# A transformer layer with routed experts on one core: eight expert tiles between the last attention pieces, routing batches of 4, 2 and 2

## What is computed

```python
x = x + self_attention(layernorm(x))             # 16 heads of 16, rotary embedding on 8 of each 16
x = x + cross_attention(layernorm(x), ctx, mask) # 16 heads, values and keys are ctx itself
x = x + experts(layernorm(x))
# experts: 8 of them, 256 -> 1024 -> 256, exact gelu; each token goes to its best two
router = x @ router_w.T + router_b + 0.1 * language_weights
top_p, top_i = top_k(softmax(router), 2);  top_p /= top_p.sum()
out = sum_k top_p[k] * (gelu(x @ w1[top_i[k]] + b1) @ w2[top_i[k]] + b2)
```

## Time and profile before

| | |
|---|---|
| median of 3 runs | 758.14 us (757.3 to 761.05) |
| the profiled execution | 760.69 us, span 758.7 us |
| PE busy | 644.1 us, 85% of the span |
| ACT, DVE, POOL busy | 53%, 46%, 38% |
| mean granted clock of PE | 0.928 |

### The profile page before, as it was taken

How to read it: one execution, slowest core, us unless ns; L and a number is a source line. 1 busy time by engine, 2 the same in 40 slices (tenths; PEclk the granted TensorE clock), 3 DMA queues, 4 the chain that set the end, 5 groups by cost and what they waited for, 6 DMA issues and landing times.

```text
span 758.7 us, 15126 instructions
## 1 busy us (share of the span) xinstructions
PE 644.1 (85%) x4858; PEld 515.5 (68%) x4858; DVE 348.7 (46%) x793; ACT 401.5 (53%) x870; POOL 284.9 (38%) x543
## 2 busy tenths in 40 slices
PE   4476798798998989999977413999999999999996
PEld 3354576475766666666634313999999999999995
DVE  1386777586786877777751440121211212212121
ACT  3443657467575777777654122545455454454551
POOL 3232305335144464643247352233324334243332
PEclk9697999899999999999998555999999999999998
DMA  5637466546677577776957901222222122221221
GB/s 127 132 96 153 96 136 150 138 121 148 134 175 157 141 152 163 178 186 143 308 131 141 226 29 37 23 37 44 31 41 42 29 43 36 36 43 29 43 30 21
DMA packets 57596, 78.25 MB, mean 103 GB/s; under 512 B 12877, under 2 KB 51152, under 8 KB 54448
## 3 DMA queue, kind: packets, MB, share of 16 engines
q1 hardware_dynamic: 48552, 66.61, 38.2%
q0 software_dynamic: 8512, 10.26, 8.6%
q10 hardware_dynamic: 456, 0.42, 0.2%
HBM read 54.52 MB, written 22.35 MB: 101 GB/s over the span
## 4 chain that ended last, share of the span: by engine, by line
PE 56%; DMA 11%; POOL 11%; issue 8%; SPq 7%; DVE 4%; ACT 3%; POOLq 0%; DVEq 0%; ACTq 0%
PE experts_psum L1218 19%; PE experts_psum L1232 17%; DMA xs<-in_x 5%; PE attention_psum L572 4%; POOL lists L1060 4%; PE attention_psum L532 4%; PE attention_psum L601 4%; PE attention_psum L545 3%; SPq L437 3%; DMA weights<-parts 2%; PE attention_psum L483 2%; POOL weights L1111 2%; SPq L443 1%; POOL rstd L1033 1%; PE experts_psum L1206 1%
## 5 line engine op out<-in xcount | busy, mean ns | idle before, releaser
L895 DVE TENSOR_REDUCE neg_max<-attention_psum 128x2 f32<-128x512 f32 x256 | 167.3, 684 | 57.7 <-PE attention_psum L532 57.3
L683 ACT ACTIVATE weights<-attention_psum 128x512 f32<-128x512 f32 x256 | 149.4, 596 | 68.2 <-PE attention_psum L545 67.2
L1218 PE MATMUL experts_psum<-xT,w1t 128*128 128x128 f32 x1248 | 146.9, 276 | 0.0
L1218 PEld LDWEIGHTS experts_psum<-xT,w1t 128*128 128x128 f32 x1248 | 143.8, 193 | 0.1
L1232 PE MATMUL experts_psum<-weights,hidT 128*128 x624 | 141.0, 379 | 0.0
L1270 ACT ACTIVATE hidT<-experts_psum,b_sb 128x128 f32<-128x128 f32 x312 | 89.6, 369 | 85.7 <-PE experts_psum L1218 85.6
L1361 POOL DMA_INDIRECT out<-y_gated,list x39 | 62.3, 1596 | 179.6 <-DVE y_gated L1335 176.5
L1232 PEld LDWEIGHTS experts_psum<-weights,hidT 128*128 128x128 f32 x624 | 115.7, 190 | 14.1
L532 PE MATMUL attention_psum<-weights 99*128 99x256 bf16 x512 | 101.9, 282 | 23.3 <-DMA weights<-parts 12.4
L1330 DVE TENSOR_TENSOR y<-experts_psum,b_sb 128x256 f32<-128x256 f32 x39 | 16.6, 425 | 207.6 <-PE experts_psum L1232 207.6
L545 PE MATMUL attention_psum<-weights 102*128 102x256 bf16 x512 | 101.3, 281 | 1.6 <-ACT weights L683 1.0
(11 more groups left out here) (158 smaller groups left out, 709.2 us busy)
## 6 DMA issues: line engine op xcount, KB each, us to landing
parts<-weights SPq DMA_DIRECT2D x96, 128.0 KB
weights<-parts SPq DMA_DIRECT2D x32, 384.0 KB
weights<-parts SPq DMA_DIRECT2D x32, 256.0 KB
weights<-in_L_ffn_w SPq DMA_DIRECT2D x8, 1024.0 KB, 11.9
weights<-parts SPq DMA_DIRECT2D x32, 128.0 KB
w_sb<-in_L_ffn_w SPq DMA_DIRECT2D x8, 512.0 KB, 3.7
weights<-in_L_ffn_w SPq DMA_DIRECT2D x8, 512.0 KB, 8.3
xs<-in_x SPq DMA_DIRECT2D x8, 256.0 KB, 8.1
```

The costliest lines, as they stand in the source:

```text
L683: act.activation(m.p[:, u % P_RING, :], m.b_bank[u % B_RING], ACT.Exp, scale=SCALE[ORDER[u // H][0]]).then_inc(m.b_free[u % B_RING], 1)
L895: v.tensor_reduce(m.neg_max[:, :, h:h + 1], m.a_bank[u % A_RING].rearrange("p (t k) -> p t k", t=T), AXX, ALU.max, negate=True).then_inc(m ...
L1218: last = pe.matmul(r.hT_bank[j % 2][:, c * P:(c + 1) * P], r.w1t[j % 2][:, k, c * P:(c + 1) * P], r.xT[j % 2][:, k, :], start=(k == 0), st ...
```

## The change

**Batches** end after cross units 3, 5 and 7: eight, four and four tiles. The list writes of the first stand in slots 240 to 254, two in every second slot, those of the second in 272 to 278, those of the third all in 304.

**Two tables.** After the first batch the kernel takes only full tiles of 128: at least eight exist, whatever the routing. DVE computes the table of these eight in slot 241, and that of the other 31 in slot 304, from the final counts less what the eight have taken.

**One stream.** The experts' functions are gone; their parts are pieces too (`TILES_AT`), placed by hand between slots 261 and 304, and from slot 304 on one tile per slot in the old order. `up` and `down` are cut into halves. The list writes of each batch have a semaphore of their own, the stores of the first four sequences too, so that the early tiles wait only for these.

**Memory.** The experts' buffers lie over attention's: w1's copies over the values, the hidden rows over the first four sequences' `xs`, the other rows over constants of attention; the banks of up are the four score banks, and the x transposes and down's results use the attention ring of three banks. Because down's end has to free a ring bank and to tell ACT, PE signals the second by an instruction of its own (`pe.sem_inc`).

```diff
-BATCH_ENDS = (5, 7, 8)
+BATCH_ENDS = (4, 6, 8)
+EARLY = 8
+assert BATCH_ENDS[0] * S * TOPK - E * (P - 1) > (EARLY - 1) * P
-AFTER_BATCH = ((39, "softmax"), (39, "soft_exp"), (40, "choose"), (42, "count"), (42, "gate_exp"), (43, "gates"), (43, "places"))
-LISTED_AT, LISTED_EVERY = 44, 2
+AFTER_BATCH = (((39, "softmax"), (39, "soft_exp"), (40, "choose"), (42, "count"), (42, "gate_exp"), (43, "gates"),
+                (43, "places"), (44, "counted"), (45, "table")),
+               ((39, "softmax"), (39, "soft_exp"), (40, "choose"), (42, "count"), (42, "gate_exp"), (43, "gates"),
+                (43, "places")),
+               ((39, "softmax"), (39, "soft_exp"), (40, "choose"), (40, "gate_exp"), (42, "count"), (43, "gates"),
+                (43, "places"), (44, "counted"), (44, "table")))
+LISTED_AT = ((44, 2), (44, 2), (44, 0))
+TILES_AT = ((261, "list", 0), (261, "list", 1), (261, "list", 2), (261, "list", 3), (262, "w1t", 0),
+            (264, "list", 4), (264, "list", 5), (264, "list", 6), (264, "list", 7),
+            (264, "gather", 0), (264, "gather", 1), (264, "gather", 2), (268, "xturn", 0), (270, "xturn", 1),
+            (272, "gather", 3), (274, "gather", 4), (276, "gelu_table", 0), (277, "up_a", 0), (277, "w1t", 1), (282, "up_b", 0),
+            (284, "up_a", 1), (285, "w1t", 2), (285, "xturn", 2), (287, "gather", 5), (288, "up_b", 1),
+            (288, "down_a", 0), (288, "down_b", 0), (292, "moved_y", 0), (292, "w1t", 3), (293, "xturn", 3),
+            (294, "gather", 6), (295, "add", 0), (297, "up_a", 2), (298, "up_b", 2), (299, "down_a", 1),
+            (299, "down_b", 1), (301, "up_a", 3), (301, "moved_y", 1), (301, "xturn", 4), (301, "w1t", 4),
+            (302, "up_b", 3), (302, "add", 1), (303, "gather", 7), (303, "down_a", 2), (303, "down_b", 2),
+            (304, "moved_y", 2), (304, "add", 2))
+STEADY, STEADY_AT = 3, 304
...
+    for j in range(STEADY, N_TILES):
+        for name, ahead in (("list", 4), ("gather", 4), ("w1t", 2), ("xturn", 2), ("up_a", 1), ("up_b", 1),
+                            ("down_a", 0), ("down_b", 0), ("moved_y", 0), ("add", 0)):
+            for k in range(j + ahead, j + ahead + 1):
+                if k < N_TILES and (name not in ("list", "gather") or k > EARLY + 1):
+                    slots[STEADY_AT + j - STEADY].pieces.append((name, TILE, k))
+            if name == "list" and j == EARLY - 4:
+                slots[STEADY_AT + j - STEADY].pieces += [(name, TILE, EARLY), (name, TILE, EARLY + 1)]
+            if name == "gather" and j in (EARLY - 3, EARLY - 2):
+                slots[STEADY_AT + j - STEADY].pieces.append((name, TILE, j + 3))
...
+            elif name == "list":
+                if n == 0:
+                    sp.wait_ge(m.s_listed[0], 16 * TOPK * T * BATCH_ENDS[0])
+                    sp.wait_ge(m.s_routed, 1)
+                if n == EARLY:
+                    for b in range(1, len(BATCH_ENDS)):
+                        sp.wait_ge(m.s_listed[b], 16 * TOPK * T * (BATCH_ENDS[b] - BATCH_ENDS[b - 1]))
+                    sp.wait_ge(m.s_routed, 2)
...
+            elif name == "up_a":
+                if n == 0:
+                    for w in range(A_RING):
+                        pe.wait_ge(m.a_free[w], len(ORDER) * H // A_RING)
+                if n == 1:
+                    for w in range(B_RING):
+                        pe.wait_ge(m.b_free[w], len(ORDER) * H // B_RING)
+                pe.wait_ge(*m.emptied(("xturn", TILE, n)))
...
+                up(n, 0)
+            elif name == "down_a":
+                if n == 0:
+                    pe.wait_ge(m.s_w2, 16 * E)
...
+            elif name == "down_b":
+                pe.wait_ge(m.s_gelu, 2 * n + 2)
+                down(n, 1, expert).then_inc(m.fills(("down_a", TILE, n)), 1)
+                pe.sem_inc(m.s_down, 1)
...
+            elif name == "gelu_table":
+                act.activation(m.scratch[:, :], m.half[:, 0:1], ACT.Gelu)
+            elif name == "w1t":
...
+                if n < 2:
+                    act.wait_ge(m.s_values, (len(ORDER) - V_RING // 2 * (1 - n)) * H)
+                else:
+                    act.wait_ge(m.s_up, 2 * (n - 1))
...
+            elif name == "gather":
+                pool.wait_ge(m.s_list[n % LIST_RING], 16 * (n // LIST_RING + 1))
...
+                if n >= X_RING:
+                    pool.wait_ge(*m.filled(("xturn", TILE, n - X_RING)))
+            elif name == "add":
...
+                pool.wait_ge(m.s_gated, n + 1)
+                if n > 0:
+                    pool.wait_ge(m.s_add, 16 * n)
```

More of the change, by code:

```diff
@@ L181, in schedule @@
         for table, lag in (((SELF_AT, CROSS_AT)[a], 0), (BOTH_AT, 0), ((AFTER_SELF, AFTER_CROSS)[a], LAG), (AFTER, LAG)):
-            for at, *piece in table + (AFTER_BATCH if table is AFTER_CROSS and n + 1 in BATCH_ENDS else ()):
+            if table is AFTER_CROSS and n + 1 in BATCH_ENDS:
+                table = table + AFTER_BATCH[batch_of(n)[0]]
+            for at, *piece in table:
                 if piece[0] != "x" or n > 1:
@@ L309, in for_attention, with for_experts @@
         self.o_bank = banks[:, 7, :]
+        self.hT_bank = [banks[:, b:b + 2, :].rearrange("p b n -> p (b n)")
+                        for b in (RING_BANKS, RING_BANKS + A_RING)]
+    def for_experts(self):
+        rows = Arena(self.over)
+        self.x_rows, self.xT = [rows([P, D]) for _ in range(X_RING)], [rows([P, KC, P]) for _ in range(2)]
+        self.y, self.y_gated = rows([P, D]), [rows([P, D]) for _ in range(2)]
+        self.list = rows([P, N_TILES, 2])
+        self.tile_expert, self.tile_row = rows([P, N_TILES], I32), rows([P, N_TILES], I32)
+        self.expert_f, self.skipped = rows([P, N_TILES]), rows([P, N_TILES])
+        self.past, self.skip = rows([P, N_TILES, E - 1]), rows([P, N_TILES, E - 1])
+        self.tiles_i, self.tiles_i2 = rows([P, E], I32), rows([P, E], I32)
+        self.tiles, self.ends, self.gap, self.full = (rows([P, E]) for _ in range(4))
+        self.early = rows([P, E + 1])
+        self.sums = rows([P, E, E])
+        heads = Arena(self.all_v)
+        self.w1t = [heads([P, KC, F]) for _ in range(2)]
+        stored = Arena(self.xs[:, 0:BATCH_ENDS[0] * T, :].rearrange("p n d -> p (n d)"))
+        self.hidT = [stored([P, FC, P]) for _ in range(2)]
     def signals(self):
@@ L332, in signals @@
         self.s_ctx_load = [sem(f"ctx_load{i}") for i in range(2)]
-        self.s_out, self.s_rows = sem("stored_out"), sem("stored_rows")
+        self.s_out, self.s_rows = ([sem(f"stored_{x}{i}") for i in range(2)] for x in ("out", "rows"))
         self.s_dve, self.s_pool = sem("dve_chain"), sem("pool_chain")
@@ L356, in fills, with stored @@
         return self.ring_full[self.plan.use[piece] % RING_BANKS]
+    def stored(self, sems, n):
+        first = BATCH_ENDS[0] if n >= BATCH_ENDS[0] else 0
+        return sems[n >= BATCH_ENDS[0]], 16 * (n - first + 1)
     def rows_of(self, n):
@@ L367, in sync_attention @@
 def sync_attention(m, x, ctx_in, mask, wq, bq, wk, bk, wv, bv, wo, bo, w_fc, router_w, router_b, lang_w, lang_b,
-                   w1, b1, w2, b2, rope, out, rows, parts, neg):
+                   w1, b1, w2, b2, rope, out, rows, parts, neg, table):
     sp, plan = m.nc.sync, m.plan
@@ L574, in values, with up, down @@
         last.then_inc(m.s_values, TOGETHER)
+    def up(j, half):
+        for c in range(half * FC // 2, (half + 1) * FC // 2):
+            for k in range(KC):
+                last = pe.matmul(m.hT_bank[j % 2][:, c * P:(c + 1) * P], m.w1t[j % 2][:, k, c * P:(c + 1) * P],
+                                 m.xT[j % 2][:, k, :], start=(k == 0), stop=(k == KC - 1))
+        last.then_inc(m.s_up, 1)
+    def down(j, half, expert):
+        for c in range(half * FC // 2, (half + 1) * FC // 2):
+            last = pe.matmul(m.bank_of(("down_a", TILE, j))[:, 0:D], m.hidT[j % 2][:, c, :],
+                             m.w2_sb[:, bass.ds(expert, 1), c, :].rearrange("p a n -> p (a n)"),
+                             start=(c == 0), stop=(c == FC - 1))
+        return last
     for slot in plan.slots:
@@ L867, in gates @@
         chain.done(v.tensor_scalar(m.total[:, tiles], m.ratio[:, tiles], 1.0, None, ALU.add))
-        then(v.tensor_tensor, m.before[:, b + 1, :], m.before[:, b, :], m.batch[:, :], ALU.add)
-        m.routed = chain.n
+        v.wait_ge(chain.sem, chain.n)
+        v.tensor_tensor(m.before[:, b + 1, :], m.before[:, b, :], m.batch[:, :], ALU.add).then_inc(m.s_before, 1)
         then(v.reciprocal, gate[0], m.total[:, tiles])
@@ L990, in vector_attention, with pool_attention @@
                                 ALU.add).then_inc(m.frees(piece), 1)
-def pool_attention(m, table):
+def pool_attention(m, table, rows, out):
     pool, plan = m.nc.gpsimd, m.plan
@@ L1377, in build @@
         sync_attention(m, x, ctx_in, mask, wq, bq, wk, bk, wv, bv, wo, bo, w_fc, router_w, router_b, lang_w, lang_b,
-                       w1, b1, w2, b2, rope, out, rows, parts, neg)
```

(3 more changed lines are left out.)

417 lines of the change are left out of this document (193 added, 224 removed).

## The result

The changed kernel took 747.87 us (median of 4 runs, 746.08 to 749.77), the kernel before, run beside it, 758.30 us (757.3 to 761.05): ratio 0.9857, 95% interval 0.982 to 0.9895. That is 10.4 us faster, where 26 were forecast, and outside the range at its upper end. The profiled execution took 748.79 us (2.0 us around its span of 746.8), 11.9 us less than the one of before.

What follows compares the result with a forecast made beforehand. PE was taken to bound the experts' stretch at 7.25 us a tile, so only tiles computed before 468 us gain. Steps 1 to 5 gave 495.3 − 469.4 = 25.9 us off 758.14: 732 us forecast, range 719 to 746.

Steps and rivals of the forecast that it cites:

- Step 1: First batch's choice and early table among the scores: PE comes 4.8 us late to slot 250, at 382.5 us.
- Step 2: List writes delay POOL in slot 250: PE waits 8.9 us, plus 2.3 at lower clock; slot 258 at 403.1.
- Step 3: Slots 258 to 276: 20.4 us (17 to 23), ending at 423.5 us.
- Step 4: Tail up to the first down: down 0 waits for w2, starts at 446.9 us and ends at 450.4.
- Step 5: From down 0's end to the transpose of tile 5: 19.0 us, reaching it at 469.4 us.
- S: Time of the transpose of tile 5, first instruction of the steady order: forecast 469.4 us, 495.3 in the old kernel.
- Covered, with 1 us to spare: Last batch's lists: gather 8 can be back at about 490 us, PE wants it at 491.2.
- An up would wait about 1 us once: Experts' buffers over attention's: without cover an up waits for a copy, about 1 us once; costed at nothing.
- POOL does not hold up the scores: List writes keep ahead and the wait in slot 250 is 0: 721 us; chance 0.20.
- the rival of chance 0.25: The clock stays low as far as the transpose of tile 5: 744 us; chance 0.25.
- A price on every tile: The extra signal at each down's end costs up to 0.87 us on each of 39 tiles: 766 us; chance 0.05.
- It does not do what it says: PE waits for late data ahead of tile 0, w2 or lists; early tiles run after the hole: 758 us; chance 0.03.

Runs made afterwards that it cites:

- e1: Changed kernel with the first batch's list writes spread around POOL's parts of the maxima; ratio to before 0.9804.
- e12: Kernel of e7 with six of the last batch's eight list writes left out; 740.55 us, ratio to before 0.969.
- e5: Changed kernel with every early-tile piece from slot 272 on put 29 slots later, behind the last unit; 753.72 us, ratio to before 0.9854.
- e9: Kernel before with only its batch ends changed, to 4, 6, 8; 770.65 us against 764.4, ratio 1.0074.
- e11: Changed kernel with the last four w2 blocks ahead of the stores and gathers 8 and 9 one step earlier; 745.54 us, ratio to before 0.974.
- e7: Changed kernel with last four w2 blocks and gathers 8 and 9 earlier, and down 2's result copied ahead of the late table; 745.33 us, ratio 0.9735.
- e14: Kernel of e7 run again as control on chip E; 745.35 us, ratio to before 0.9734.
- e13: Kernel of e7 with the last batch's list writes split, four in slot 304 and four in 305, behind add 3; ratio to before 0.9748.
- c2: The changed kernel unaltered, run on chip D; 753.12 us, ratio to before 0.9828.
- e2: Changed kernel with the last four blocks of w2 issued ahead of the stores of cross unit 6; ratio to before 0.9756.
- e8: Kernel of e7 with two more blocks of w2 earlier, in slot 260; 748.34 us, ratio to before 0.9758.

## Why the prediction was wrong, point by point

**Step 1** had the choice right (a wait of 2.82 us at 365.05, moved and not added). Its price for the early table was too low: the table cost a wait of 3.36 us and not 1.7, and the clock was at 0.67 between 366 and 374 us, behind the wait of 2.82 us; PE arrived at slot 250 at 386.8 us (392.73 − 5.90) and not at 382.5. **Step 2** was right in its mechanism and its place (slot 250 at 391.4 forecast, 392.73 measured), and its wait was 5.9 us and not 8.9, since PE came later. That slot 258 met the forecast so well (403.1 and 402.85) is in part luck: it came 10.1 us behind slot 250 where 9.4 + 2.3 were charged, which made up for the 1.3 us that slot 250 was late. In e1 taking POOL's wait away won 3.0 to 3.4 us, since other waits stand beside it. **Step 3**: the last values began at 424.28 us where 423.5 was forecast.

**Step 4** had the mechanism right and its terms too small. PE's own time was met (ready at 444.8 us, 444.0 forecast), and the last block of w2 released down 0. But down 0 was to start at 446.9 and end at 450.4; it started at 451.56 and was followed by the transposes of tile 3 at 457.60, 7.2 us late. Of that, 1.7 us are the later issue (433.67 for 432.0), 1.9 the landing (16.80 for 14.9), 1.1 the way from landing to first product, and 2.5 the half clock (6.04 us for 3.5). I had taken the landing of one pair as a constant. The same line of the kernel before shows that it is none: two blocks issued 11 us earlier landed after 12.0 and 18.7 us.

```profile
L462 SPq DMA_DIRECT2D weights<-in_L_ffn_w x2: 372/481/590, 411.1 to 411.5; - x2
...
DMA to landing us min/median/max: 12.0/15.3/18.7
```

In the changed kernel the last pair took 13.7 and 16.8 us. And I had charged no clock behind the wait, having put only 2.9 us of waiting there.

**Step 5's** 19.0 us were right: 457.60 to 476.73 are 19.1. The two table loads of ACT took 1.28 us each there (at 465.85 and 471.01 us). So S was late by just those 7.3 us.

**The loop** failed in kind: its cover at tile 8 and at the ring bank was not there. "Covered, with 1 us to spare": gather 8 was to be back at 490 us, wanted at 491.2. It was issued at 500.50. I had counted the list writes on POOL, and had left out the three adds that stand between them and the gather, each waiting for the landing of the last; the margin was 1 us against a queue of 14 us. It cost 3.05 us and 1.84 at a lower clock behind it (0.57 from 504 to 508 us). "An up would wait about 1 us once": it was down 3, whose ring bank is freed by a copy on DVE behind the late table, the table that I had "beside 10 us of list writes": 1.85 us. Together 6.74 us, as S to end shows (that PE's wait for w2 also was 6.74 us is chance). With the 7.3 of S that is the 14.1 us between 25.9 and 11.8. On the other chips PE's products are also held back at the list writes, which no view of before could show, as the old kernel made the last batch's writes (451.00 to 455.89 us) while PE was idle.

**The rivals.** *POOL does not hold up the scores* fell by 5.90 us of waiting; where e1 takes that wait away, 3.0 to 3.4 us are won at slot 250, and not 11, and none of it reaches the end. That the clock stays low as far as S (the rival of chance 0.25, at 744 us) fell: from 460 to 504 us the clock was 1.00. A low clock behind a wait was there in small, once in down 0 (2.5 us, at 0.58) and once behind tile 8's wait (1.8, at 0.57). *A price on every tile* fell: tiles stand 7.24 us apart at 708 us, as in the earlier trace rows, and the way from S to the end is 257.1 us in e12 and 257.3 in e5, with the extra signal, and 257.1 in e9 and in the kernel before, without it. *It does not do what it says* fell too.

## What to carry to other kernels

A step is priced by the whole queue ahead of it, the waits inside that queue included: list the instructions between the last one that you cost and the one that must be in time. A landing time read from one pair is no constant: take the range of all its like (11.8 to 18.7 us in the kernel before), and price the low clock behind a wait on top (2.5 us here behind 6.74). Run the change with its parts taken apart: here tiles that do not hang on the last batch bring the larger part, and where they are placed the smaller. The best versions here kept the change and moved the late transfers and the gather forward (e11: 745.5 us against 753.1 for the change and 765.0 before; e7 and e14 have the same ratio within noise).

## What was not expected of the hardware

- On chips B to E the kernel before took 764.2 to 765.1 us, on A 758.3; the change brought 10.4 us on A, 16.1 on C and 11.8 on D.
- Eight indirect writes of lists in a row on POOL, 1.27 us each, go with single products on PE 0.7 to 2.1 us apart on chips B to E; split four and four, or with six left out, they go with none (e13, e12 against e14). On chip A the same burst goes with none either. Waits of the same kind of 2 to 5 us, put down to nobody, stand at or just ahead of slot 250 (386 to 393 us) on those chips beside the first batch's writes. Part of them is POOL's wait under another name: in c2 POOL ends its parts at 392.10 us and PE goes on at 392.15. That the rest has the same cause as the single products was not tried.
- The half clock behind a wait does not go by its length alone. Ahead of down 0 waits of up to 3.44 us kept it at 3.7 us and the clock at 1.00 (e2, e7, e8, e11, e14), those of 5.06 us and more made it 5.6 to 6.6 us at 0.56 to 0.66; but ahead of tile 8 a wait of 2.89 us was followed by an up of 5.44 us instead of 3.74, the clock at 0.57 from 504 to 508 us.
